# The weighted sum's matmuls in another order: eight on one half of the rows, then eight on the other

## What is computed

```python
def local_attention(q, k, v):                    # b, h, n, d = q.shape; w = 32; nw = n // w
    ...
    bk2, bv2 = (look(bk), look(bv))              # each window with the one before it: 64 keys
    sim = jnp.einsum('bhwie,bhwje->bhwij', bq, bk2) * QK_SCALE
    sim = jnp.where(mask, -jnp.finfo(sim.dtype).max, sim)
    attn = jax.nn.softmax(sim, -1)
    out = jnp.einsum('bhwij,bhwje->bhwie', attn, bv2)      # the weighted sum
    return out.reshape(b, h, n, d)
```

## Time and profile before

| what | value |
|---|---|
| three runs, us | 3873.29, 3888.59, 3900.0 (median 3888.59) |
| the profiled execution's own time | 3905.88 us |
| its span, first to last instruction | 3903.7 us |
| TensorE (PE) busy | 3491.8 us, 89% of the span |
| VectorE (DVE) busy | 3004.6 us, 77% |
| GpSimd (POOL) busy | 2719.5 us, 70% |
| ScalarE (ACT) busy | 2710.9 us, 69% |
| mean granted TensorE clock | 0.952 of full |

### The profile page before, as it was taken

One profiled execution on the slowest core, in us unless ns is written; L12 is line 12 of the kernel. 1 busy time (PEld: TensorE's weight loads), 2 busy tenths in 40 slices (PEclk: granted clock), 3 DMA queues, 4 the chain that ended last, 5 costly groups with the idle time before them and its releaser, 6 DMA issues. The chain is left out here.

```text
span 3903.7 us, 159146 instructions
## 1 busy us (share of the span) xinstructions
PE 3491.8 (89%) x62588; PEld 2485.2 (64%) x62588; DVE 3004.6 (77%) x4752; ACT 2710.9 (69%) x7080; POOL 2719.5 (70%) x3091
## 2 busy tenths in 40 slices
PE   8799999999999999985555789999999999999996
PEld 3577777777777777762111367777777777777774
DVE  7678788787787888855888778878778787778883
ACT  2478787787877787763434468777777777777874
POOL 4578787777787787850334478777778787777872
PEclk9899999999999999996778889999999999999998
DMA  1223332333333333320000023333333333332331
GB/s 40 61 69 77 76 83 69 83 75 73 80 72 79 78 75 77 78 53 16 0 0 0 21 68 77 77 81 73 76 73 76 75 76 74 80 76 68 88 71 37
DMA packets 183174, 252.07 MB, mean 65 GB/s; under 512 B 53659, under 2 KB 74783, under 8 KB 182303
## 3 DMA queue, kind: packets, MB, share of 16 engines
q1 hardware_dynamic: 182422, 241.71, 26.0%
HBM read 39.13 MB, written 1.05 MB: 10 GB/s over the span
## 5 line engine op out<-in xcount | busy, mean ns | idle before, releaser
L860 POOL TENSOR_TENSOR qk_rows<-rot_products 128x512 f32<-128x512 f32 x768 | 983.3, 1282 | 244.9 <-DVE rot_products L659 242.4
L659 DVE TENSOR_TENSOR rot_products<-psum,rot_scaled 128x1024 f32<-128x1024 f32 x768 | 937.4, 1221 | 162.1 <-ACT squares L470 117.9
L870 POOL TENSOR_TENSOR qk_rows<-qk_rows,rnorm 128x512 f32<-128x512 f32 x768 | 803.3, 1078 | 15.0
L266 PE MATMUL psum<-wqkv_hi,xs_hi 128*128 (+1 forms) x1152 | 561.9, 488 | 92.0 <-DVE rot_products L659 47.3
L470 ACT ACTIVATE squares<-psum 128x512 f32<-128x512 f32 x768 | 487.7, 635 | 73.5 <-PE psum L268 60.8
L661 DVE TENSOR_REDUCE sumsq<-squares 128x8 f32<-128x512 f32 x768 | 518.7, 675 | 0.0
L835 POOL TENSOR_TENSOR probs<-probs,rden 128x512 f32<-128x512 f32 x384 | 393.2, 1046 | 107.1 <-DVE rden L709 106.4
L514 ACT ACTIVATE probs<-psum,minus_row_max 128x64 f32<-128x64 f32 x1536 | 458.5, 336 | 5.9 <-DVE minus_row_max L693 5.8
L268 PE MATMUL psum<-wqkv_hi,xs_lo 128*128 (+1 forms) x1152 | 462.0, 401 | 0.0
L267 PE MATMUL psum<-wqkv_lo,xs_hi 128*128 (+1 forms) x1152 | 461.1, 400 | 0.0
L328 PEld LDWEIGHTS psum<-probs_t,v_pairs 64*64 64x64 f32 x24576 | 390.7, 136 | 106.7 <-issue 106.3
(11 more groups left out here) (159 smaller groups left out, 6081.7 us busy)
## 6 DMA issues: line engine op xcount, KB each, us to landing
v_pairs<-v_rows SPq DMA_DIRECT2D x3072, 64.0 KB
wqkv_staged<-in_Wqkv SPq DMA_DIRECT2D x52, 384.0 KB, 3.4
wo<-in_Wo SPq DMA_DIRECT2D x12, 512.0 KB, 4.2
w<-in_W SPq DMA_DIRECT2D x12, 341.0 KB, 3.2
qk_scale<-in_qk_scale SPq DMA_DIRECT2D x12, 128.0 KB, 3.2
w<-in_W SPq DMA_DIRECT2D x12, 128.0 KB
rot_base<-in_rot SPq DMA_DIRECT2D x2, 512.0 KB, 3.6
out_x<-qk_rows SPq DMA_DIRECT2D x1, 1024.0 KB, 5.7
```

Source lines behind the costliest of these rows:

```text
L266: nc.tensor.matmul(proj_ps[c % 2], xh, wh, start=True, stop=False)
L659: V.tensor_tensor(m["mm"][:, c % 2, :, :].rearrange("p a (h e) -> p a h e", e=DH), ps, cos_sin, ALU.mult)\
L860: G.tensor_tensor(qk[:, c * CH:(c + 1) * CH].rearrange(half, a=2, e=DH // 2), cos, sin[:, :, ::-1, :], ALU.add)\
L870: G.tensor_tensor(part, part, m["rn"][:, u % 2, HC * c:HC * c + HC].unsqueeze(2) .to_broadcast([P, HC, DH]), ALU.mult).then_inc(S["rot_don ...
```

## The change

The three inner loops of `pe_pv` stand in another order. Before, `par` is the innermost, so the halves of the rows alternate. After, `par` is outside the windows `w` and the column halves `j`. The 64 matmuls, their operands, their outputs and their flags are the same. The two increments of `o_mm` stay with the last matmul of either half; the one of par = 0 now comes eight matmuls before that of par = 1.

```diff
         def pe_pv(it, u, half):
 
             for hp in range(4 * half, 4 * half + 4, 2):
-                for w in range(WPT):
-                    for j in range(2):
-                        for par in range(2):
+                for par in range(2):
+                    for w in range(WPT):
+                        for j in range(2):
                             rows = slice(64 * par, 64 * par + 64)
                             last = nc.tensor.matmul(
                                 o_ps[par][64 * j:64 * j + 64, P * (hp // 2) + WIN * w:P * (hp // 2) + WIN * w + WIN],
```

## The result

The changed kernel takes 3909.05 us (median of 12 runs, 3897.57 to 3923.7), the kernel before 3887.85 us in the same set (12 runs): a ratio of 1.0051, 95% interval 1.0031 to 1.0071, or about 21 us more. The forecast was 3921 us, 32 us more than the median shown then. The profiled execution of the changed kernel has a span of 3914.9 us, 11.2 us more than before.

The account below looks back on a forecast made before the run. TensorE, 95% busy in the layer phases, was taken to bound the kernel; 192 units x 0.22 us = 42 us, less 10 given back, made +32 us: 3921 us on the median's scale, range 3870 to 4070 us.

Parts of the forecast that it names:

- likeliest case: Weighted sum: two quarters fall behind once per unit, a small lag; +15 to +48 us, 3903 to 3937 us; chance 0.50.
- the halves take turns: Rival, weighted sum: a full quarter queue holds up all behind; block 0.70 us, +179 us, 4058 us; wholly or partly 0.25.
- What bounds the kernel: TensorE, 95% busy in the layer phases; in the weighted sum each of four quarters takes one record per 0.059 us.
- Step (a): Weighted sum, block start: 16 matmuls stand ready, so all four quarters start together and the block still takes 0.47 us.
- window of 64 entries: TensorE's window by the skill page: two loads and two matmuls for each of 16 matmuls, said to agree with the scores' burst.
- hidden loads: Rival, weighted sum: weight loads hide behind the stream; -177 us at most, partially -69 us, 3820 us; chance 0.10.
- Step (b): Weighted sum, next block: places free in order on completion, so two quarters lag once, 0.22 us per unit, 42 us in all.
- the even start: Weighted sum before the change: even groups of four from the start, read as several matmuls standing ready per quarter.
- Step (c): TensorE's waits for other engines give back 10 us of the 42; waits for `o_t` and late-instruction holes count nothing.

Follow-up runs that it names:

- order by columns: Kernel before with the column halves outermost in the weighted sum, so eight matmuls run on one column half, then eight on the other: ratio 1.0019, run again 1.0017.
- order by rows: The changed kernel itself: eight matmuls on one half of the rows, then eight on the other; ratio 1.0051 to the kernel before, run again 1.0072.
- runs of four: Kernel before with the weighted sum reordered to four matmuls on one half of the rows, then four on the other, two to each quarter: ratio 1.0012.
- quarters one at a time: Kernel before with the weighted sum reordered to four matmuls in a row on each quarter of the array in turn: 4196.23 us, ratio 1.0775.
- runs of sixteen: Kernel before with the weighted sum reordered to sixteen matmuls on one half of the rows, then sixteen on the other, twice per unit: ratio 1.0301.

## Why the prediction was right, and where it was not

The number held: +32 us were forecast, +21 (12 to 28 by the interval) measured, and it is inside the likeliest case's own range. But that is luck: it came out right by two errors of opposite sign, and what happened in the array is the rival "the halves take turns" in its partial form, whose sign (two records in the first 0.05 us) is the one that appeared. The signs of the likeliest case did not: four records at the start, a unit of 2.29 us and 460 us for L328 were forecast, and two records, 2.52 us and 504.6 us came.

- **What bounds the kernel.** Right as to the unit: four quarters, one record per 0.058 us each. All measured units of the weighted sum follow within 0.06 us from that step, a depth of two and the 0.02 to 0.03 us to enter.
- **Step (a) failed.** "If any of them can go when its quarter is free, B and D start with A and C": they start four records late. I had read the burst of 32 records in the earlier trace rows as 16 places for all. It is two places before each of the eight pieces of the scores, and the row can't tell these apart, because the scores go round all eight. Nor does it bear out the window of 64 entries, as the prediction had it: these 16 matmuls are what eight pieces hold, whatever the window. For four quarters the same depth makes eight places. The hint of hidden loads in the same row falls too: that burst is one record per 0.056 us on each of eight pieces, no faster than a quarter's 0.058.
- **Step (b) had the right form and the wrong size.** A lag once per unit, 0.19 to 0.25 us, was forecast; the first lag is 0.25 us, but by the full queue and not by finished records, and each later block adds 0.067 us, so a unit grows by 0.45 us and not by 0.22. TensorE's group grew by 86.4 us, not by 42.
- **The rival "the halves take turns"** was nearer in mechanism: it had the queue before each quarter and the hold-up. Its point, "fewer than about four records", was too low: with room for just four records the block of eight on a quarter does lose time. Its price of 0.70 us per block stood on a depth of two records; with four it is 0.533. I also held the even start against it, which it fits.
- **The skill's rule.** The Trainium skill, "TensorE: Matmul & The Clock Gate", Part 3, "What overlaps and what doesn't", ties the overlap to different row groups. The order by columns, with neighbours on different row halves, has the same 2.52 us unit as the order by rows, and runs of four on one half lose 0.02 us a unit. These runs do not agree with it for tiled matmuls, matmuls on pieces of the array. Nor do they with the strict program order that the prediction quotes from there: B's first record starts at 0.266 us, ahead of the last three of A, whose matmuls stand before it in the program.
- **Step (c) failed, on the other side.** I gave back 10 us. Of 67.8 us more busy time 56.6 us were given back in the profiled execution. The prediction's own sign against (c), a kernel that grows by under half of what its units grow by, appeared: 21 of 86 us. The wait rows of the changed kernel, beside the earlier trace rows:

```profile
PE psum L266 <- DVE rot_products L659: 30.3, 25, 3.9
PE psum L266 <- ACT gelu L534: 21.0, 19, 2.0
PE psum L363 <- ACT o_t L486: 11.5, 12, 2.5
PE psum L328 <- issue: 8.8, 23, 0.9
```

The waits for `rot_products` fell by 17.0 us, those for `o_t` by 17.2, the holes in L328 by 18.4, and those for gelu rose by 6.8: 45.8 of the 56.6 us. "`o_t` moves with it, so those 28.7 us give nothing" was wrong. ScalarE stood idle for the weighted sum in only 2 of 192 units before. In the others it came to the copy into `o_t` straight from its own earlier work, so a weighted sum that ends a little later did not move the copy. The same row of the changed kernel, then that of the run with quarters one at a time, where the copy does wait in every unit:

```profile
  ACT o_t L486: 7.1, 5
```

```profile
  ACT o_t L486: 183.7, 192
```

Counting the holes at nothing was wrong as well, and their size was misread. The 133.5 us over 295 places add the idle time before the weight loads, 106.3 us, to that before the matmuls, 27.2 us. A weight load that starts late while matmuls still run is no hole in TensorE's work. The holes before the matmuls are the 27.2 us, and 18.4 of them went.

The larger delays show where that ends. Against the runs of four of the same set (span 3883.5 us, PE busy 3478.8), runs of sixteen are busy 217 us longer and last 119 us longer, and quarters one at a time are busy 413 us longer and last 310 us longer. So 57, 99 and 103 us are given back for 68, 217 and 413 us of added work: a stock that runs out at about 100 us, after which nearly all is paid. In the last of these kernels 5.0 us of PE's waits for `o_t` are left, and no "issue" hole in front of the L328 matmuls.

At the same clock the changed kernel costs 12 us and the order by columns 13 to 15 us. So some of the 21 us of the result may be the clock's and not the queue's; how many is open, since the clock of the kernel before is not on record for those runs.

## What to carry to other kernels

When TensorE works in pieces of its array, go round the pieces in program order and never put more than two fp32 matmuls on one piece before the others have had theirs: in these runs two in a row were nearly free (0.02 to 0.06 us per unit of 64), three cost 0.14 us, four 0.45 and eight 1.25. No run tried longer streams or other sizes than these two. A burst in a trace shows the total that stands ready, not how it is shared out, so read the depth per piece only from a stretch that repeats a piece. Price a delay of the busiest engine by its waits and by the holes before its instructions: of the growth of the units, 86 us, a quarter reached the kernel (21 us); of 476 us, with quarters one at a time, 302; and a unit with 16 matmuls more was paid in full. And when two kernels differ by half a per cent, lay their runs over the granted clock first: here 0.01 of it was worth 34 to 38 us, more than the whole change.

## What was not expected of the hardware

A matmul for an idle quarter is held up by one for a busy quarter, two matmuls deep, although the two records of one matmul are freely passed by those of others. At the granted clock of 0.50 the step of a record is 0.108 us against 0.059, so it is bound by the clock. With one quarter at work, loads and matmuls start in turn, 0.026 to 0.030 us apart: the step holds a load and a stream one behind the other. And two kernels with the same work, the same unit and the same busy time of TensorE differed by 0.5%, together with a granted clock of 0.946 against 0.953; over all runs of three sets the time followed the granted clock by 34 to 38 us per 0.01, nearly the 39 us of half of 2% of the time.
